# Linear attention in a fused kernel: the halves of the query heads are added on GpSimd one unit ahead, VectorE sums 256 columns, and the memory term goes between units

## The reference, cut to what matters

```python
def _L0_conv_ref(x, g, w_qkv, mem_kv, w_out, b_out):      # HEADS = 4, DIM_HEAD = 32
    norm = jnp.maximum(jnp.sqrt(jnp.sum(x * x, axis=1, keepdims=True)), 1e-12)
    xn = x / norm * g[None, :, None, None] * C ** 0.5
    q, k, v = jnp.split(jnp.einsum('bchw,oc->bohw', xn, w_qkv), 3, axis=1)
    ...                                                    # to (b, heads, dh, n), n = 256
    k = jnp.concatenate([mk, k], axis=-1)                  # 4 memory columns per head
    v = jnp.concatenate([mv, v], axis=-1)
    q = jax.nn.softmax(q, axis=-2) * scale                 # over the 32 of a head
    k = jax.nn.softmax(k, axis=-1)                         # over the positions
    context = jnp.einsum('bhdn,bhen->bhde', k, v)
    out = jnp.einsum('bhde,bhdn->bhen', context, q)
    return jnp.einsum('bchw,oc->bohw', out.reshape(b, hidden, H, W), w_out) + b_out[...]
...
x = x + _L0_conv_ref(_gn(x), ...)
```

## Time and profile before

| | |
|---|---|
| median of 3 runs | 572.61 us (571.94 to 576.02) |
| profiled execution, time | 572.74 us |
| profiled execution, span | 570.9 us |
| mean granted TensorE clock | 0.956 |
| busy share PE, DVE, ACT, POOL | 88%, 72%, 55%, 28% |

### The profile page before, as it was taken

The page is one execution under the profiler, slowest core; times in us unless marked ns, Lnnn a source line. Parts: engine busy times, 40 slices in busy tenths (PEclk is TensorE's granted clock), DMA queues, the critical chain, the costliest instruction groups (busy, mean ns, idle before and its releaser), DMA issues. The chain is left out here.

```text
span 570.9 us, 15184 instructions
## 1 busy us (share of the span) xinstructions
PE 503.4 (88%) x6313; PEld 293.7 (51%) x6313; DVE 409.6 (72%) x751; ACT 311.7 (55%) x543; POOL 158.4 (28%) x210
## 2 busy tenths in 40 slices
PE   8957778999888889989888878989999999999993
PEld 3547654466665553255555544444664566366520
DVE  5758978686444589967788857975786776777664
ACT  3255635243344310267988875355776577667573
POOL 0106423000000000043565640000692078038600
PEclk9976899999999879999999999979999999999998
DMA  8400007000000075000000000000000000000002
GB/s 262 47 6 3 3 2 242 1 2 1 2 1 2 1 175 121 0 3 1 2 1 2 3 20 2 0 8 13 1 3 6 8 2 1 12 2 2 1 7 77
DMA packets 22560, 15.02 MB, mean 26 GB/s; under 512 B 17466, under 2 KB 20570, under 8 KB 22363
## 3 DMA queue, kind: packets, MB, share of 16 engines
q1 hardware_dynamic: 22490, 14.00, 9.8%
HBM read 8.71 MB, written 1.08 MB: 17 GB/s over the span
## 5 line engine op out<-in xcount | busy, mean ns | idle before, releaser
L2327 DVE TENSOR_REDUCE R<-ps 128x4 f32<-128x1024 f32 x48 | 56.6, 1221 | 21.3 <-PE ps L1849 20.9
L2150 ACT ACTIVATE R<-ps 128x512 f32<-128x512 f32 x96 | 52.0, 597 | 11.0 <-PE ps L1861 10.9
L2233 POOL TENSOR_TENSOR R<-R 128x512 f32<-128x512 f32 x42 | 53.3, 1270 | 16.4 <-ACT R L2150 16.4
L1609 POOL TENSOR_TENSOR R<-R 128x512 f32<-128x512 f32 x32 | 45.4, 1417 | 39.8 <-DVE R L1542 39.8
L1542 DVE TENSOR_TENSOR R<-ps,lasting 128x512 f32<-128x512 f32 x64 | 41.1, 685 | 11.7 <-PE ps L1464 11.7
L1861 PE MATMUL ps<-tmpA,R 32*128 32x256 f32 x384 | 48.3, 378 | 0.0
L1576 ACT ACTIVATE R<-R 128x1536 f32<-128x1536 f32 x32 | 47.3, 1479 | 0.1
L1849 PE MATMUL ps<-R,tmpA 32*128 32x256 f32 x384 | 45.4, 392 | 0.0
L1464 PE MATMUL ps<-R,Q 32*128 32x128 f32 (+1 forms) x512 | 29.9, 346 | 10.0 <-ACT R L1592 10.0
L1861 PEld LDWEIGHTS ps<-tmpA,R 32*128 32x128 f32 x384 | 36.5, 185 | 0.5
L1464 PEld LDWEIGHTS ps<-R,Q 32*128 32x128 f32 x512 | 23.9, 184 | 20.8 <-DVE R L1542 16.9
(11 more groups left out here) (336 smaller groups left out, 1103.9 us busy)
## 6 DMA issues: line engine op xcount, KB each, us to landing
R<-z SPq DMA_DIRECT2D x32, 128.0 KB, 2.4
R<-in_qv SPq DMA_DIRECT2D x1, 2560.0 KB
x<-in_x SPq DMA_DIRECT2D x4, 256.0 KB, 3.5
out<-x SPq DMA_DIRECT2D x4, 256.0 KB, 2.6
lasting<-in_lasting SPq DMA_DIRECT2D x1, 811.0 KB, 8.4
early<-in_early SPq DMA_DIRECT2D x1, 793.5 KB, 7.0
scatter<-in_scatter SPq DMA_DIRECT2D x1, 512.0 KB, 5.4
P<-scratch_w SPq DMA_DIRECT2D x16, 32.0 KB, 2.6
```

The source lines that it names most:

```text
L1609: pool.tensor_tensor(diagonal(u), diagonal(u), diagonal(u), ALU.mult).then_inc(diag_squared[1], 1)
L2150: act.activation(m.et[:, g % 2, j, :], ps[:, turned_bank(g, j), :], ACT.Exp)\
L2233: pool.tensor_tensor(m.esum[:, g % 2, two, :], m.et[:, g % 2, two, 0:N], m.et[:, g % 2, two, N:2 * N], ALU.add).then_inc(sg["halves_added" ...
L2327: dve.tensor_reduce(m.parts[:, g % 2, :, a:a + 2, 3 * g].rearrange("p s i -> p i s"), ps[:, a:a + 2, :].rearrange("p i (s m) -> p i s m", ...
```

## The change

GpSimd gets a new operation for each unit, `add_halves(u)`: it waits for the unit's exponential and, from unit 2 on, for the sum of unit u - 2, adds columns 0 to 15 of each head to columns 16 to 31, and writes the 256 results to `q_halves(u)`, one of two buffers in columns 768 to 1279 of `z`. VectorE's sum now waits for that instead of the exponential and reads the 256 columns. GpSimd's order becomes: add 0, then for each u: add u + 1, multiply u. The two halves of the memory term leave their place ahead of the multiplications and come ahead of the addition of unit u + 1 at u = 3 and u = 4. No DMA and no other engine's program changes.

```diff
--- before.py
+++ after.py
@@ -311,6 +311,7 @@
     qmax_ready = sem("la_qmax_ready")
     qsub_done = sem("la_qsub_done")
     qexp_done = sem("la_qexp_done")
+    qhalves_added = sem("la_qhalves_added")
     qsum_ready = sem("la_qsum_ready")
     qinv_ready = sem("la_qinv_ready")
     qnorm_done = sem("la_qnorm_done")
@@ -346,6 +347,10 @@
 
     def q_stat(t, u):
         return t[:, 16 * u:16 * u + 16]
+
+    def q_halves(u):
+        at = 768 + u % 2 * 256
+        return m.z[:, at:at + 256].rearrange("p (j h d) -> p j h d", j=J, h=HEADS)
 
     BY_V = (11, 13, 15)
 
@@ -577,8 +582,8 @@
                                   ALU.subtract).then_inc(qsub_done, 1)
 
             def invert_sums(u):
-                dve.wait_ge(qexp_done, u + 1)
-                dve.tensor_reduce(by_head(q_stat(m.qsum, u)), q_unit(u), AXX, ALU.add).then_inc(qsum_ready, 1)
+                dve.wait_ge(qhalves_added, u + 1)
+                dve.tensor_reduce(by_head(q_stat(m.qsum, u)), q_halves(u), AXX, ALU.add).then_inc(qsum_ready, 1)
                 dve.wait_ge(qsum_ready, u + 1)
                 dve.reciprocal(q_stat(m.qinv, u), q_stat(m.qsum, u)).then_inc(qinv_ready, 1)
 
@@ -745,17 +750,30 @@
             pool.tensor_copy(part[1], left).then_inc(parts, 1)
             pool.wait_ge(parts, 3)
             pool.tensor_tensor(part[2], left, part[1], ALU.subtract).then_inc(parts, 1)
-            pool.wait_ge(f_done, 1)
-            pool.wait_ge(w2mem_copied, 1)
-
-            for half in range(2):
+
+            def memory_terms(half):
+                if half == 0:
+                    pool.wait_ge(f_done, 1)
+                    pool.wait_ge(w2mem_copied, 1)
                 g = slice(half * G // 2, (half + 1) * G // 2)
                 pool.tensor_tensor(m.kmem[:, half * B // 2:(half + 1) * B // 2, :].rearrange("p (g j) c -> p g j c", j=J),
                                    m.kfac[:, :].rearrange("p (j g) -> p g j", j=J)[:, g, :].unsqueeze(3)
                                    .broadcast_to([128, G // 2, J, 33]),
                                    m.w2mem[:, None, None, :].broadcast_to([128, G // 2, J, 33]),
                                    ALU.mult).then_inc(memterm, 1)
+            def add_halves(u):
+                pool.wait_ge(qexp_done, u + 1)
+                if u >= 2:
+                    pool.wait_ge(qsum_ready, u - 1)
+                pool.tensor_tensor(q_halves(u), q_unit(u)[:, :, :, 0:DH // 2], q_unit(u)[:, :, :, DH // 2:DH],
+                                   ALU.add).then_inc(qhalves_added, 1)
+
+            add_halves(0)
             for u in range(UN):
+                if u in (RND - 1, RND):
+                    memory_terms(u - RND + 1)
+                if u + 1 < UN:
+                    add_halves(u + 1)
                 pool.wait_ge(qinv_ready, u + 1)
                 pool.tensor_tensor(q_unit(u), q_unit(u), by_head(q_stat(m.qinv, u)).unsqueeze(3)
                                    .broadcast_to([128, J, HEADS, DH]), ALU.mult).then_inc(qnorm_done, 1)
```

## The result

| | before | changed |
|---|---|---|
| median | 572.56 us (20 runs) | 576.34 us (20 runs) |
| ratio, 95% interval | | 1.0064 [1.0039, 1.0090] |
| profiled execution, time | 572.74 us | 574.26 us |
| profiled execution, span | 570.9 us | 572.5 us |

The changed kernel is slower by 0.64%, 3.7 us with an interval from 2.2 to 5.2 us. A second set of runs gave 1.0050 [1.0015, 1.0085], 2.9 us. The ratios leave out the slow executions, among them one of the kernel before that took 1119 us. The loss is inside the 1% called "no change", and it has the sign of the forecast. The forecast was 574.5 us, a loss of 1.9 us, with a range of 572.0 to 577.2; the loss measured is 1.5 to 2 times as large.

The account below looks back on a forecast made before the run. TensorE's arrival at its last eight turn-overs bounds the stage, leaving the softmax 1.25 us; GpSimd's order delays exponential 15 by 3.1 us, a net +1.9 us. From 572.74 us that gives 574.6, less 0.1: 574.5 us, range 572.0 to 577.2.

Parts of the forecast that it names:

- The prices: Linear attention's query softmax: a 256-column sum on VectorE takes 0.42 us, a 256-column addition on GpSimd 0.73 us.
- The schedule: Step-by-step delays in the query softmax: units 4, 8 and 12 start 1.5, 1.9 and 3.3 us late.
- exponential 15: ScalarE's exponential of unit 15, the last query unit: starts at 75.80 us instead of 72.72, 3.1 us late.
- the gate: Start of TensorE's last eight turn-overs, at 75.09 us before; waits for ScalarE's copy of unit 6, forecast 1.9 us late.
- The idle time of VectorE: Sign: VectorE idle before most third and fourth sums of a group, about 1.1 us each, 5 us and more in all.
- The saving is worth nothing while TensorE sets the gate: Shorter sums take 3.7 us off VectorE but gain nothing, since TensorE would still arrive at 75.09 us.
- No loss to sharing: GpSimd and VectorE plainly work at once in the softmax, so nothing was added for their shared SBUF read port.
- the slack: ScalarE's copy of unit 6 ends at 73.84 us, TensorE's last eight turn-overs start at 75.09: 1.25 us to spare.
- the context sum's wait: TensorE's turn-over of unit 1 waits for VectorE's context sum, from 62.25 to about 63.0 us: 0.75 us.
- The clock rival: TensorE, waiting for copies between about 70 and 77 us, drops to the lower clock: 577.0 or 581.5 us; chance 0.08.
- the sign given for this rival: In the changed profile, TensorE's granted clock is under 1.00 after 70 us.
- swallowed: Not slower: the softmax's slack absorbs a delay of exponential 15 under 1.25 us, time 572.6 us; chance 0.18.

Follow-up runs that it names:

- half sum alone: Kernel before, with VectorE summing only the first 16 of each head's 32 entries and GpSimd adding nothing: linear-attention stage 44.07 us, against 44.18 us before.

## Why the prediction was right, and where it fell short

*The prices.* 0.73 us for an addition and 0.42 us for a sum, each from the row of its width, were right to 0.01 us, and so was the overlap: additions advance GpSimd by 0.69 us.

*The schedule.* Taken from the copy of `w2mem`, the delays at units 4, 8 and 12 were forecast as 1.5, 1.9 and 3.3 us and measured as 1.5, 1.9 and 3.4 us; exponential 15 as 3.1 and 3.1 us; the gate as 1.9 and 2.0 us. The idle time of VectorE was "5 us and more" and was 8.2 us. Of these, the places in the changed kernel are what the working earned. That the differences agree too is in part luck: they are taken from an execution of the kernel before whose own softmax was 1.2 us late, by a wait that the other execution does not have. Against that one the delays at units 4, 8 and 12 are 1.5, 3.1 and 4.6 us, and the gate's is 4.4 us.

*The saving is worth nothing while TensorE sets the gate.* Shown by the half sum alone, in an execution with the clock of the first profile; not tried with the clock up, where TensorE no longer sets it alone.

*No loss to sharing.* The Trainium skill, page "Perfetto Trace Analysis", section "Optimizing Scalar/DVE Operations", warns that work moved between GpSimd and VectorE may not help because the two share a read port of SBUF. The trace does not bear that out here: 1.046 us for a multiplication in the changed kernel, against 1.048 us. The loss came from the order in GpSimd's queue.

*The step that fell short* is the slack: "TensorE would still arrive at 75.09 us", 1.25 us behind ScalarE's copy. The size of the loss, 1.9 us, is exponential 15's 3.1 us less that slack. It was read from one execution, in which TensorE ran at the lower clock from 50 to 57 us and again from 60 to 64 us and so was late by itself. In an execution with the clock up, the kernel before has no slack at the gate (0.23 us of waiting instead) and its stage is 41.82 us. Against that one the delay of the softmax (exponential 15 at 33.8 us instead of 29.5) counts in full. The prediction also missed a path: it followed VectorE's delay to the exponentials and to the context sum, but not to the next query round, where the changed kernel waits 1.4 us and loses the clock. And it gave the context sum's wait 0.75 us, less than the gate's; in the second profile of the changed kernel that wait was 1.58 us, and TensorE came to the gate last. Two profiles each give stages of 44.2 and 41.8 us before, 46.2 and 47.1 us after; their means differ by 3.6 us, near the 3.7 and 2.9 us of the timed runs. With four executions this is a plausible account of the size and not a proof. That idleness in place of query round 2 goes with the fall of the clock is seen in five executions against three; what the fall alone costs stays open, since no run here held the wait and kept the clock.

*The clock rival* had 0.08 and put the fall at 70 to 77 us. The clock did fall, at another place, 54 to 68 us, and it was back at the full level before 70 us, so that the sign given for this rival did not appear. The *swallowed* rival had 0.18 and falls: the loss is clear of the noise in both sets of runs.

## What to carry to other kernels

When work moves to a second engine, draw that engine's queue and not only its load: here GpSimd had the time, and an addition behind a multiplication still made VectorE wait for eight microseconds to save four. Put what another engine waits for, for a whole round, ahead of what nobody waits for yet. And read a slack from more than one execution: one that consists of another engine's lower clock is gone when the clock is up. When two profiles are compared, first find how far their granted clocks go the same way.

## What was unexpected of the hardware

The same program's stage took 44.18 and 41.82 us in two executions, with the same instructions; what differs first is TensorE's granted clock (0.50, 0.66, 0.76 and 0.81 in four successive 4 us windows, against 1.00). In the first it fell at 49.8 us, inside an idle time of 2.06 us that the second has at the same place and of the same length, without a fall: the same idle time did not decide by itself. The time ahead of the copy of `w2mem` also varied, from 41.6 to 47.3 us over the 14 profiles, which is more than anything the change does, and is one reason why whole runs of this kernel tell so little.
